# Cross attention: value products of four key tiles at a time, with twelve places for probabilities instead of two tiles and eight places

## The chip, the core and the metric

The kernel runs on one core of a Trainium2 chip. The metric is the device time of one execution in microseconds (us); lower is better. TensorE (PE) multiplies matrices into PSUM, VectorE (DVE) and ScalarE (ACT) read PSUM, GpSimd (POOL) works in SBUF only, SyncE (SP) issues transfers.

## The reference, cut to what matters

Four layers follow one another for a batch of 4, each with 256 tokens of width 256. The change lies in the third layer, in its cross attention with 16 heads of 8 dimensions over the 1601 context rows:

```
ci = rms_norm(hidden_states, ln_post_cross_w)
cq = heads(ci @ cq_w, NH, CHD)                      # 16 heads x 8
ck, cv = split(encoder_outputs @ ckv_w)             # encoder_outputs: 1601 rows x 128
scores = einsum('bhqd,bhkd->bhqk', q * scale, k)
p = softmax(scores, axis=-1)
cctx = einsum('bhqk,bhkd->bhqd', p, v)
hidden_states = hidden_states + cctx @ cdense_w
```

The batches are computed one after the other.

## The kernel before

The program is written out by hand, engine by engine, with semaphores between them. In the cross attention the 16 heads are worked in four groups of four (`gr` = 0 to 3), and the 1601 keys in 13 tiles of 128 (`KT` = 13). Within a group a key tile `kt` has two units (`u` = 0, 1), one for each two heads, so a group has 26 units, numbered `n` = 26 `gr` + 2 `kt` + `u`. In this text "score 11 of group 1" is unit 11 of that group.

For each unit, TensorE makes the scores, keys on partitions and 2 x 256 queries in the columns, in one matmul with a 128-column weight tile (`st<-cq_blocks,ck_stack`, or `x<-cq_blocks,ck_stack`) into one of three PSUM banks (`st_bank`). ScalarE takes the exponential into one of the places for probabilities (`slot(n)`: 4 in `prob`, 4 in `prob2`; in the profile `probs` and `probs_cross`). TensorE multiplies the probabilities with the values of the tile (`cross_pv`, `pv<-probs,v_cross` or `pv<-probs_cross,v_cross`), with weight tiles of 32 columns, into 32 partitions of `PV` for each head. One such float32 product stands as two rows in the trace, so the products of two key tiles are 16 rows and those of four tiles 32 rows.

The shift by the row maximum has to be known before a group starts. So behind every score matmul of group `gr` stands one matmul of another pass (`cross_max`, `x<-ck_stack,cq_blocks`), the scores of group `gr`+1 or `gr`+2 with queries on partitions, into one of three banks (`max_bank`), and VectorE reduces it (L1876, for the short last tile L1878). There are 26 of these for a group and they run 5 ahead (`LEAD`), so that the last one of all stands behind score 20 of group 2; group 3 has none.

In TensorE's order a step of the loop over `k0` takes two key tiles: four scores, each with its maximum matmul, and then the value products of the two tiles before. Other work stands in between:

- Queries: in groups 0 and 1, behind score 7, TensorE makes the query blocks of group `gr`+2 (`mi<-cq_hi,const_r`), and ScalarE copies them out behind exponential 7 (L794, four pieces).
- Shifts: before score 24 of groups 0 to 2, TensorE transposes the negated maxima (L1355), and ScalarE writes them into the query blocks (L801, four pieces) before its exponential 24. The next group's first score waits for them (`sc_set`).
- In group 3, behind score 11, four rows of a selector product (`x<-ctx_heads_t,const_f`) on the first three groups' results.
- A score waits for the exponential three units back, a maximum matmul for the reduction three back, and an exponential for a free place.

Of the kernel before, what the change touches and what calls it, by code (L numbers as in the profile page):

```python
# [15 lines left out]
F32 = mybir.dt.float32  # L16
# [7 lines left out]
P = 128  # L24
# [115 lines left out]
def program(nc, io):  # L140

    with ExitStack() as ctx:
        top = [nc.sbuf_base]

        def place(name, shape, dt, where):
            size = int(np.prod(shape[1:])) * (1 if dt == U8 else 4)
            off = -(-where[0] // 64) * 64
            where[0] = off + size
            return nc.alloc_sbuf_tensor_at(name, shape, dt, offset=off)

        def sb(name, shape, dt=F32):
            return place(name, shape, dt, top)
# [4 lines left out]
        def sig(name, per=1, primed=False):  # L157
            return Signal(ctx.enter_context(nc.semaphore(name)), per, primed)
# [20 lines left out]
        prob = sb("probs", [P, 4, 512])  # L179
        x0 = sb("x_in", [P, TT, D])  # L180
        xa, xb, xn = sb("x_a", [P, TT, D]), sb("x_b", [P, TT, D]), sb("x_normed", [P, TT, D])
# [82 lines left out]
        prob2 = place("probs_cross", [P, 4, 512], F32, e)  # L264
# [22 lines left out]
        wd = place("w_dense", [P, 2, 4, D], F32, w)  # L287
        z = [late]
        wgu = place("w_gate_up", [P, 2, DC, 2, FIP], F32, z)
        assert max(a[0], w[0], z[0]) <= nc.sbuf_usable_end  # L290


# [50 lines left out]
        sc_mm, pc_exp, pvc_mm = sig("sc_mm", 8 * KT), sig("pc_exp", 8 * KT, primed=True), sig("pvc_mm", 8 * KT, primed=True)  # L343
# [35 lines left out]
        def st_bank(n):  # L379

            return (ST[0][:], ST[1][:], half_bank(3))[n % 3]

        def slot(n):

            return prob[:, n % 8] if n % 8 < 4 else prob2[:, n % 8 - 4]

        block = ctx.enter_context(nc.Block())

# [210 lines left out]
        def _(act):  # L599
# [45 lines left out]
            def body(b, more):  # L645
# [143 lines left out]
                def cross_queries(gr):  # L789

                    act.wait_ge(qg_mm.handle, qg_mm.at(b * 4 + gr))
                    for h in range(4):
                        r = slice(32 * h, 32 * h + 32)
                        m = act.activation(qb2[gr % 3][r, h], MI[r, 0:NT], ACT.Identity, bias=ck[r, K_Q_CROSS:K_Q_CROSS + 1])  # L794
                    m.then_inc(qg_read.handle, 1)

                def cross_shifts(gr):

                    act.wait_ge(nmc_t.handle, nmc_t.at(b * 4 + gr))
                    for h in range(4):  # L800
                        m = act.activation(qb2[gr % 3][32 * h:32 * h + 4, h], MI[0:4, NT:2 * NT], ACT.Copy)  # L801
                    m.then_inc(sc_set.handle, 1)

                def cross_out(gr):

                    act.wait_ge(pvc_mm.handle, pvc_mm.at(b, 2 * KT * (gr + 1)))
                    act.activation(cx[:, gr], PV[:, 0:NT], ACT.Copy).then_inc(cc_read.handle, 1)
# [4 lines left out]
                for gr in range(4):  # L812
                    for k in range(2 * KT):
                        n = 2 * KT * gr + k
                        if gr < 3 and k == 24:
                            cross_shifts(gr + 1)
                        act.wait_ge(sc_mm.handle, sc_mm.at(b, n + 1))
                        act.wait_ge(pvc_mm.handle, pvc_mm.at(b, max(0, n - 7)))
                        act.activation(slot(n), st_bank(n), ACT.Exp, scale=float(HC2) ** -0.5).then_inc(pc_exp.handle, 1)  # L819
                        if gr and k == 3:  # L820
                            cross_out(gr - 1)
                        if gr < 2 and k == 7:
                            cross_queries(gr + 2)
# [10 lines left out]
            for b in range(B):  # L834
                body(b, b < B - 1)

        @block.tensor
        def _(pe):
            prime(pe, down_mm, sum_mm, pv_mm, pvs_mm, pvc_mm)
            def mm(out, lhsT, rhs, start=True, stop=True):  # L840
                return pe.matmul(out, lhsT, rhs, start=start, stop=stop, skip_group_check=True)  # L841
# [112 lines left out]
            def body(b, more):  # L954
# [264 lines left out]
                for m2 in range(2):  # L1219
                    for k in range(4):  # L1220
                        n = 0
# [5 lines left out]
                for t in range(TT):  # L1227
                    n = 0
# [105 lines left out]
                def cross_max(g):  # L1334

                    if g == 4 * CPARTS:
                        return
                    gr, m, bank = g // CPARTS, g % CPARTS, max_bank(g)
                    qt, h, c = m // 13, m % 13 // 3, m % 13 % 3
                    if m == 0:  # L1340
                        pe.wait_ge(qg_read.handle, qg_read.at(b * 4 + gr))
                    if g >= 3:
                        pe.wait_ge(mc2_read.handle, mc2_read.at(b, g - 2))
                    if m % 13 < 12:
                        t = mm(bank, qb2[gr % 3][:, h, qt * P:(qt + 1) * P], ks2[gr][:, c * 512:(c + 1) * 512])
                    else:
                        for h in range(4):
                            t = mm(bank[:, h * HEADW:(h + 1) * HEADW], qb2[gr % 3][:, h, qt * P:(qt + 1) * P], ks2[gr][:, 1536:1536 + HEADW])
                    t.then_inc(mc2_mm.handle, 1)

                def cross_shifts(gr):
                    pe.wait_ge(nmc.handle, nmc.at(b * 4 + gr))
                    pe.wait_ge(qg_read.handle, qg_read.at(b * 4 + min(gr + 1, 3)))
                    for qt in range(TT):
                        m = pe.transpose(MI[0:4, NT + qt * P:NT + (qt + 1) * P], nmx[:, qt, :], ident)  # L1355
                    m.then_inc(nmc_t.handle, 1)

                def cross_pv(gr, kt):

                    for u in range(2):  # L1360
                        n = 2 * KT * gr + 2 * kt + u
                        pe.wait_ge(pc_exp.handle, pc_exp.at(b, n + 1))
                        if kt == 0 and u == 0:
                            pe.wait_ge(cc_read.handle, cc_read.at(b * 4 + gr, 0))
                        for h in range(2):
                            hd = 2 * u + h
                            m = mm(PV[32 * hd:32 * hd + 32, 0:NT], vx[:, kt, VXW * (4 * gr + hd):VXW * (4 * gr + hd) + 32],
                                   slot(n)[:, h * NT:(h + 1) * NT], kt == 0, kt == KT - 1)
                        m.then_inc(pvc_mm.handle, 1)
# [7 lines left out]
                for gr in range(4):  # L1377
                    pe.wait_ge(sc_set.handle, sc_set.at(b * 4 + gr))
                    for k0 in range(0, KT, 2):
                        if k0 == 12 and gr < 3:  # L1380
                            cross_shifts(gr + 1)
                        for kt in range(k0, min(k0 + 2, KT)):
                            for u in range(2):
                                n = 2 * KT * gr + 2 * kt + u
                                pe.wait_ge(pc_exp.handle, pc_exp.at(b, max(0, n - 2)))
                                m = mm(st_bank(n), ks2[gr][:, kt * P:(kt + 1) * P],
                                       qb2[gr % 3][:, 2 * u:2 * u + 2].rearrange("p h n -> p (h n)"))
                                m.then_inc(sc_mm.handle, 1)
                                if g < 4 * CPARTS:
                                    cross_max(g)  # L1390
                                    g += 1
                        if gr < 2 and k0 == 2:
                            cross_queries(gr + 2)
                        if gr == 3 and k0 == 4:
                            pe.wait_ge(cc_read.handle, cc_read.at(b * 4 + 2))
                            mm(X[0][:, 0:512], cc[:, C_SELC], cx[:, 0:2].rearrange("p k n -> p (k n)"))
                            mm(X[0][:, 512:512 + NT], cc[:, C_SELC], cx[:, 2]).then_inc(cc_sum.handle, 1)
                        if k0:
                            cross_pv(gr, k0 - 2)
                            cross_pv(gr, k0 - 1)  # L1400
                        elif gr:
                            cross_pv(gr - 1, KT - 1)
                cross_pv(3, KT - 1)
                pe.wait_ge(cc_read.handle, cc_read.at(b * 4 + 3))
                mm(X[1][:, 0:NT], cc[:, C_SELC], cx[:, 3]).then_inc(cc_sum.handle, 1)
# [10 lines left out]
                for k in range(6):  # L1416
# [3 lines left out]
                    for gu in range(2):  # L1420
                        n = 0
# [6 lines left out]
                for t in range(TT):  # L1428
                    n = 0
# [10 lines left out]
            for b in range(B):  # L1440
                body(b, b < B - 1)
# [569 lines left out]
```

## Time and profile before

| | |
|---|---|
| median of 3 runs | 2308.95 us (2303.93 to 2312.57) |
| profiled execution, its own time | 2304.52 us |
| its span | 2302.7 us |
| TensorE busy | 87% |
| VectorE, ScalarE, GpSimd busy | 56%, 40%, 33% |
| mean granted TensorE clock | 0.921 |

The profile is of one execution. Its rows give the start from the beginning of the span, the duration, the engine, the line in the kernel, the operation and the tiles it writes and reads. "PEld" are the weight loads of TensorE, which can run beside its matmuls. Matmuls are pipelined, so the time that one costs is read from start to start, not from its duration.

### The profile page before, as it was taken

The page shows a single profiled execution, that of the slowest core. Times are in us where ns is not written, and L with a number is a line of the kernel's source. Part 1 is how long each engine was busy: PE and PEld are TensorE (multiplying, and loading weights), DVE is VectorE, ACT ScalarE, POOL GpSimd, SP SyncE. Part 2 cuts the span into 40 slices and gives each one's busy share as a digit, 9 for nine tenths or more (in the row PEclk, how much of TensorE's full clock was granted, in tenths as well). Part 3 has the DMA queues.
Part 4 walks back from the last instruction along what each step waited for, and adds up shares of the span by engine and source line. Part 5 has one row for each costly group of instructions (what it writes and reads, how often), then busy time and mean ns, then how long its engine had stood idle before and what let it go on. Part 6 is the DMA issues. An engine that isn't in the chain of part 4 may idle for free.

```text
span 2302.7 us, 30843 instructions
## 1 busy us (share of the span) xinstructions
PE 2004.1 (87%) x11940; PEld 1485.0 (64%) x11940; DVE 1298.0 (56%) x2045; ACT 923.0 (40%) x1718; POOL 766.9 (33%) x676
## 2 busy tenths in 40 slices
PE   3999888898899978899889988889888998888986
PEld 2676667556677657655676766765577765775655
DVE  5666335664676623675576753367457664346733
ACT  1455232371355413257045541326415553231731
POOL 3678410000378731000237881100025886100000
PEclk9999999799899999879999998988999999887998
DMA  4000200201000020100100001020010001102000
GB/s 177 9 11 5 112 1 1 83 1 43 29 12 8 12 104 1 42 41 1 48 26 14 8 37 76 1 83 1 23 36 20 10 8 69 44 1 82 1 1 5
DMA packets 18145, 74.16 MB, mean 32 GB/s; under 512 B 2896, under 2 KB 10320, under 8 KB 14544
## 3 DMA queue, kind: packets, MB, share of 16 engines
q1 hardware_dynamic: 17424, 69.56, 8.2%
q10 hardware_dynamic: 576, 2.62, 0.3%
q8 instruction: 96, 1.57, 0.3%
q14 instruction: 49, 0.40, 0.1%
HBM read 71.13 MB, written 1.05 MB: 31 GB/s over the span
## 4 chain that ended last, share of the span: by engine, by line
PE 68%; DVE 17%; ACT 7%; issue 5%; POOL 2%; DMA 1%; SPq 0%; ACTq 0%; POOLq 0%; DVEq 0%
PE x L841 27%; PE pv L841 18%; PE st L841 15%; PE mi L841 6%; DVE k_hi_lo L1459 3%; ACT k_hi_lo L612 2%; DVE max_parts L1540 2%; POOL prob_sums L555 1%; ACT probs L657 1%; DVE q_lo_shift L1549 1%; DVE prob_sums L1847 1%; PE x L965 1%; DVE x_normed L1640 1%; DVE w_pair_lo L1459 1%; ACT ck_stack L745 1%
## 5 line engine op out<-in xcount | busy, mean ns | idle before, releaser
L555 POOL TENSOR_TENSOR prob_sums<-prob_sums,probs 128x512 f32<-128x512 f32 x352 | 453.6, 1289 | 65.0 <-ACT probs L657 19.0
L657 ACT ACTIVATE probs<-st 128x512 f32<-128x512 f32 x416 | 228.5, 596 | 294.4 <-PE st L841 290.8
L1540 DVE TENSOR_REDUCE max_parts<-x 128x1 f32<-128x832 f32 x256 | 250.7, 1020 | 128.6 <-PE x L841 127.4
L539 POOL TENSOR_TENSOR rstd_work<-rstd_work 128x2 f32<-128x2 f32 x24 | 16.7, 695 | 796.4 <-DVE rstd_work L1456 796.4
L1876 DVE TENSOR_REDUCE max_cross<-x 128x1 f32<-128x512 f32 x384 | 238.8, 684 | 72.0 <-PE x L841 70.5
L841 PE MATMUL st<-q_hi_hi,k_hi_lo 128*128 128x256 f32 x832 | 231.2, 309 | 17.6 <-DVE q_lo_shift L1549 17.6
L841 PE MATMUL pv<-probs,v 128*64 128x256 f32 x1664 | 231.6, 397 | 3.7 <-DVE recip_sum L1664 3.7
L841 PEld LDWEIGHTS st<-q_hi_hi,k_hi_lo 128*128 128x128 f32 x832 | 159.9, 192 | 95.5 <-issue 86.2
L841 PE MATMUL st<-q_lo_shift,k_hi_rows 128*128 128x256 f32 x832 | 210.8, 285 | 0.0
L841 PE MATMUL x<-ck_stack,cq_blocks 128*128 128x512 f32 (+1 forms) x512 | 196.4, 458 | 0.1
L841 PEld LDWEIGHTS st<-q_lo_shift,k_hi_rows 128*128 128x128 f32 x832 | 160.7, 193 | 0.1
L1459 DVE TENSOR_TENSOR k_hi_lo<-x,k_hi_lo 64x832 fp32r<-64x832 f32 x128 | 131.0, 1023 | 40.6 <-ACT k_hi_lo L612 39.3
L841 PEld LDWEIGHTS pv<-probs,v 128*64 128x64 f32 x1664 | 101.1, 137 | 81.5 <-issue 27.1
L841 PE MATMUL x<-k_hi_rows,q_hi 128*128 128x416 f32 x512 | 128.9, 361 | 20.3 <-DVE k_hi_lo L1459 17.6
L841 PEld LDWEIGHTS x<-ck_stack,cq_blocks 128*128 128x128 f32 x512 | 107.6, 226 | 43.8 <-DVE max_cross L1876 32.2
L841 PE MATMUL st<-cq_blocks,ck_stack 128*128 128x512 f32 x280 | 121.6, 443 | 10.6 <-ACT cq_blocks L801 6.5
L1664 DVE RECIPROCAL recip_sum<-pv 128x256 f32<-128x256 f32 x32 | 56.2, 1757 | 108.8 <-PE pv L841 108.8
L612 ACT ACTIVATE k_hi_lo<-x 64x832 fp32r<-64x832 f32 x128 | 110.0, 859 | 17.6 <-PE x L841 15.9
L493 POOL TENSOR_SCALAR k_hi_rows<-k_hi_lo 64x1664 fp32r<-64x1664 f32 x64 | 101.0, 1579 | 38.6 <-ACT k_hi_lo L612 35.7
L841 PEld LDWEIGHTS x<-k_hi_rows,q_hi 128*128 128x128 f32 x512 | 85.3, 190 | 32.9 <-issue 28.9
L819 ACT ACTIVATE probs<-st 128x512 f32<-128x512 f32 x140 | 80.3, 604 | 28.4 <-PE st L841 27.9
L841 PEld LDWEIGHTS st<-cq_blocks,ck_stack 128*128 128x128 f32 x280 | 53.7, 194 | 56.5 <-ACT probs_cross L819 17.1
(291 smaller groups left out, 4158.0 us busy)
## 6 DMA issues: line engine op xcount, KB each, us to landing
w_gate_up<-in_wgu SPq DMA_DIRECT2D x4, 3072.0 KB, 10.1
w_ff<-in_w SPq DMA_DIRECT2D x8, 1024.0 KB, 5.7
w_qk<-in_wqk SPq DMA_DIRECT2D x4, 2048.0 KB, 9.0
w_pair<-in_w SPq DMA_DIRECT2D x32, 192.0 KB, 2.3
w_down<-in_wdn SPq DMA_DIRECT2D x4, 1536.0 KB, 13.4
w_dense<-in_wd SPq DMA_DIRECT2D x4, 1024.0 KB, 12.2
mask_ints<-in_mask SPq DMA_DIRECT2D x4, 832.0 KB, 4.3
ctx_t_raw<-in_ctxT SPq DMA_DIRECT2D x4, 832.0 KB, 5.3
```

The costliest lines, as they stand in the source:

```text
L493: pool.tensor_scalar(t["kh1"][0:64, :, c], r32(t["kst"][0:64, :, c]), 1.0, 0.0, ALU.mult, ALU.add)\
L555: pool.tensor_tensor(acc[:, 0], acc[:, 0], prob[:, kt % 4], ALU.add).then_inc(add_pool.handle, 1)
L612: act.activation(par[s]["kst"][0:64, h, j * HALF:(j + 1) * HALF].rearrange("p (c n) -> p c n", c=2), X[j][64 * h:64 * h + 64, :].rearrange ...
L657: act.activation(prob[:, kt % 4], ST[kt % 2][:], ACT.Exp, scale=HD0 ** -0.5).then_inc(p_exp.handle, 1)
L745: act.activation(ks2[gr][:, j * HALF:j * HALF + n], X[j][:, 0:n], ACT.Identity, bias=ck[:, K_OH_CROSS:K_OH_CROSS + 1])\
L819: act.activation(slot(n), st_bank(n), ACT.Exp, scale=float(HC2) ** -0.5).then_inc(pc_exp.handle, 1)
L841: return pe.matmul(out, lhsT, rhs, start=start, stop=stop, skip_group_check=True)
L965: last = pe.transpose(X[0][:, o:o + P], src[:, t, ch * P:(ch + 1) * P], ident)
L1459: return dve.tensor_tensor(out, x, y, op)
L1540: dve.tensor_reduce(mxs[:, qt, h, half:half + 1], X[n % 2][:].rearrange("p (c n) -> p c n", c=2)[:, :, 0:QUART], AX.XY, ALU.max).then_inc( ...
L1664: dve.reciprocal(rec[:], PV[:, NT:2 * NT]).then_inc(recip.handle, 1)
L1876: t = dve.tensor_reduce(mxc[:, qt, h, c:c + 1], bank, AX.X, ALU.max)
```

## The change

The value products are issued four key tiles at a time (behind the scores of tiles 5, 9 and 12) instead of two at a time (behind those of tiles 3, 5, 7, 9, 11 and 12). Those of tile 12 stay behind the first four scores of the next group. The places for probabilities grow from eight to twelve: two in a new tile `probs_cross_late`, and the tiles `x_in` (`x0`) and `x_normed` (`xn`), which nothing else uses during this stage. The exponential's wait for a free place goes from eight units back to twelve back.

```
@@ places @@
         wgu = place("w_gate_up", [P, 2, DC, 2, FIP], F32, z)
+        prob3 = place("probs_cross_late", [P, 2, 512], F32, z)
@@ slot(n) @@
-            return prob[:, n % 8] if n % 8 < 4 else prob2[:, n % 8 - 4]
+            n %= 12
+            if n < 8:
+                return prob[:, n] if n < 4 else prob2[:, n - 4]
+            return prob3[:, n - 8] if n < 10 else (x0, xn)[n - 10][:].rearrange("p t d -> p (t d)")
@@ ScalarE @@
                         act.wait_ge(sc_mm.handle, sc_mm.at(b, n + 1))
-                        act.wait_ge(pvc_mm.handle, pvc_mm.at(b, max(0, n - 7)))
+                        act.wait_ge(pvc_mm.handle, pvc_mm.at(b, max(0, n - 11)))
@@ TensorE @@
-                        if k0:
-                            cross_pv(gr, k0 - 2)
-                            cross_pv(gr, k0 - 1)
-                        elif gr:
+                        if k0 == 0 and gr:
                             cross_pv(gr - 1, KT - 1)
+                        if k0 and k0 % 4 == 0:
+                            for kt in range(k0 - 4, k0):
+                                cross_pv(gr, kt)
```

The first place is on TensorE in group 1, from the query blocks behind score 7 to score 12. Before, `cq_blocks_153` and `ck_stack_160` being this group's operands:

```order
L841 MATMUL mi<-cq_lo,const_r 128x256
L841 MATMUL pv<-probs,v_cross 32x256 x4
L841 MATMUL pv<-probs_cross,v_cross 32x256 x4
L841 MATMUL st<-cq_blocks_153,ck_stack_160 128x512
L841 MATMUL x<-ck_stack_161,cq_blocks_154 128x512
L841 MATMUL x<-cq_blocks_153,ck_stack_160 128x512
L841 MATMUL x<-ck_stack_161,cq_blocks_154 128x512
L841 MATMUL st<-cq_blocks_153,ck_stack_160 128x512
L841 MATMUL x<-ck_stack_161,cq_blocks_154 128x512
L841 MATMUL st<-cq_blocks_153,ck_stack_160 128x512
L841 MATMUL x<-ck_stack_161,cq_blocks_154 128x512
L841 MATMUL pv<-probs_cross,v_cross 32x256 x4
```

The same place in the changed program, where L845 is the same line four further down:

```order
L845 MATMUL mi<-cq_lo,const_r 128x256
L845 MATMUL st<-cq_blocks_153,ck_stack_160 128x512
L845 MATMUL x<-ck_stack_161,cq_blocks_154 128x512
L845 MATMUL x<-cq_blocks_153,ck_stack_160 128x512
L845 MATMUL x<-ck_stack_161,cq_blocks_154 128x512
L845 MATMUL st<-cq_blocks_153,ck_stack_160 128x512
L845 MATMUL x<-ck_stack_161,cq_blocks_154 128x512
L845 MATMUL st<-cq_blocks_153,ck_stack_160 128x512
L845 MATMUL x<-ck_stack_161,cq_blocks_154 128x512
L845 MATMUL pv<-probs,v_cross 32x256 x4
L845 MATMUL pv<-probs_cross,v_cross 32x256 x8
L845 MATMUL pv<-probs_cross_late,v_cross 32x256 x4
```

The products of tiles 0 and 1 have moved from ahead of score 8 to behind score 11 and its maximum matmul, where they now stand in front of those of tiles 2 and 3.

The second place is on ScalarE at the end of group 1, from exponential 20 to exponential 4 of group 2. Its order before:

```order
L819 ACTIVATE probs<-st 128x512 x2
L819 ACTIVATE probs<-x 128x512
L819 ACTIVATE probs<-st 128x512
L801 ACTIVATE cq_blocks_152<-mi 4x256 x4
L819 ACTIVATE probs_cross<-st 128x512
```

And in the changed program:

```order
L823 ACTIVATE probs<-st 128x512 x2
L823 ACTIVATE probs<-x 128x512
L823 ACTIVATE probs<-st 128x512
L805 ACTIVATE cq_blocks_152<-mi 4x256 x4
L823 ACTIVATE probs_cross<-st 128x512
```

Nothing has moved on ScalarE here or elsewhere in the stage: the exponentials only go to other places. VectorE's order is unchanged too.

## Rows read from the trace of the kernel before

**Rows 1.** The page: the chain that ended last, shares of the span by engine

```profile
PE 68%; DVE 17%; ACT 7%; issue 5%; POOL 2%; DMA 1%; SPq 0%; ACTq 0%; POOLq 0%; DVEq 0%
```

**Rows 2.** Stretches: length, busy PE, PEld, DVE, ACT, POOL, clock, DMA share, GB/s

```profile
400.00:404.00 4.00, 4.00 (x12) 3.21 (x12) 3.80 (x2) 0.00 (x0) 0.00 (x0) 0.60 0.00 0
...
448.00:526.00 78.00, 76.02 (x615) 42.86 (x613) 47.42 (x73) 60.93 (x124) 0.00 (x0) 1.00 0.01 1
...
1011.00:1089.00 78.00, 76.04 (x615) 42.90 (x614) 47.65 (x74) 60.93 (x124) 0.00 (x0) 1.00 0.00 1
```

**Rows 3.** Timeline of group 2, a step of two key tiles

```profile
496.54 0.40 PE L841 MATMUL st<-cq_blocks,ck_stack 128*128 128x512 f32 x1
496.78 0.40 PE L841 MATMUL x<-ck_stack,cq_blocks 128*128 128x512 f32 x1
497.11 1.07 PE L841 MATMUL pv<-probs_cross,v_cross 128*32 128x256 f32 x16
498.11 0.50 PE L841 MATMUL x<-cq_blocks,ck_stack 128*128 128x512 f32 x1
498.44 0.40 PE L841 MATMUL x<-ck_stack,cq_blocks 128*128 128x512 f32 x1
...
498.88 2.48 DVE L1876 TENSOR_REDUCE max_cross<-x 128x1 f32<-128x512 f32 x4 [0.58 <-PE x L841]
...
501.16 0.50 PE L841 MATMUL st<-cq_blocks,ck_stack 128*128 128x512 f32 x1
```

**Rows 4.** Timeline of group 1 from the query blocks to score 12

```profile
470.23 0.64 PE L841 MATMUL pv<-probs,v_cross 128*32 128x256 f32 x8
...
470.36 1.90 ACT L794 ACTIVATE cq_blocks<-mi,const_cols 32x256 fp32r<-32x256 f32 x4
...
472.29 0.60 ACT L819 ACTIVATE probs<-st 128x512 f32<-128x512 f32 x1
...
472.94 0.50 PE L841 MATMUL st<-cq_blocks,ck_stack 128*128 128x512 f32 x1
...
473.60 0.64 PE L841 MATMUL pv<-probs_cross,v_cross 128*32 128x256 f32 x8
474.06 0.61 PE L841 MATMUL pv<-probs,v_cross 128*32 128x256 f32 x8
474.60 0.50 PE L841 MATMUL x<-cq_blocks,ck_stack 128*128 128x512 f32 x1
```

**Rows 5.** VectorE's reductions (ns: shortest, median, longest), and seven in a row

```profile
L1876 DVE TENSOR_REDUCE max_cross<-x x384: 677/681/693, 422.6 to 2184.8; 128x1 f32<-128x512 f32 x192
...
465.87 4.52 DVE L1876 TENSOR_REDUCE max_cross<-x 128x1 f32<-128x512 f32 x7 [0.84 <-PE x L841]
```

**Rows 6.** A step of group 3, without maximum matmuls

```profile
517.57 0.50 PE L841 MATMUL st<-cq_blocks,ck_stack 128*128 128x512 f32 x1
...
518.11 0.60 ACT L819 ACTIVATE probs_cross<-st 128x512 f32<-128x512 f32 x1 [0.56 <-PE st L841]
...
518.76 0.50 PE L841 MATMUL st<-cq_blocks,ck_stack 128*128 128x512 f32 x1 [0.21 <-ACT probs_cross L819]
...
519.08 1.09 ACT L819 ACTIVATE probs<-st 128x512 f32<-128x512 f32 x2
519.19 0.64 PE L841 MATMUL pv<-probs,v_cross 128*32 128x256 f32 x8
...
520.19 0.50 PE L841 MATMUL x<-cq_blocks,ck_stack 128*128 128x512 f32 x1
```

**Rows 7.** From group 2 to group 3: shifts, then scores 0 and 4 of group 3

```profile
504.19 1.53 ACT L801 ACTIVATE cq_blocks<-mi 4x256 fp32r<-4x256 f32 x4 [0.24 <-PE mi L1355]
...
505.76 1.12 PE L841 MATMUL st<-cq_blocks,ck_stack 128*128 128x512 f32 x2
...
508.36 0.50 PE L841 MATMUL st<-cq_blocks,ck_stack 128*128 128x512 f32 x1
```

**Rows 8.** A wait of TensorE ahead of the stage

```profile
398.58 1.13 PE L841 MATMUL mi<-ctx_heads_t,const_f 128*128 128x512 f32 x2 [1.96 <-DVE ctx_heads_t L1853]
```

## The prediction

> **What bounds the kernel now.** I read the page's chain first. TensorE carries 68% of it, VectorE 17%, ScalarE 7% [rows 1]. That is a mean over unlike stages, so the stage that the change touches has to be read by itself. In its main stretch TensorE is busy for 76.02 of 78 us at the full granted clock, ScalarE for 60.93, VectorE for 47.42; the same stretch of the next batch reads 76.04 [rows 2]. So TensorE binds, ScalarE is not far behind, four batches repeat the same pattern, and what is worked out for one counts four times.
>
> Then the timeline of one step of two key tiles. Matmuls with 128-column weights start 0.23 to 0.24 apart, but the first value product starts 0.33 behind the last of them; eight product rows take 0.46 [rows 4], yet the block of sixteen is followed by the next score only after 1.00; and the matmul behind that score comes after 0.33 [rows 3]. A change between the two forms of weight tile and back thus costs 0.10 + (1.00 - 0.92) + 0.11 = 0.29 us a block. Check: 8 x 0.23 + 0.92 + 0.29 = 3.05, and the step reads 498.11 to 501.16.
>
> **The saving.** A group has seven product blocks now and four afterwards. Three blocks fewer x 0.29 x 16 groups = 13.9 us. That is the gain if TensorE never waits longer than before. The product rows, their number and their operands' sizes stay as they are; the new places are SBUF tiles like the old ones, with no transfer to or from them in this stage, and I cost them at nothing. Exponential n waits for the products of n - 12; at every step these are issued a block earlier than needed, so this wait never ends last.
>
> What it takes is cover. In a burst TensorE now makes eight scores and eight maximum matmuls at a stretch instead of four and four, with only three banks for each, so the readers' pace shows. And ScalarE's side jobs used to lie beside product blocks. Piece by piece, for a batch:
>
> *Scores 4 to 11 of groups 0 and 1.* ScalarE copies the query blocks for 1.90 us between exponentials 7 and 8. Exponential 8 starts at 472.29 and ends at 472.89, and score 11 starts at 472.94 [rows 4]. Before, 1.00 us of products (from 470.23) lay inside that wait; now scores 8 to 10 start there at once, TensorE is done with them at about 471.7 and stands still for about 1.2 us. Score 11 cannot come earlier, since ScalarE's chain has not moved. The block behind it still starts at 473.60, with 32 rows instead of 16, so score 12 comes 0.92 later than 474.60. The saved change is lost in the wait. Two groups: +1.84.
>
> *Scores 12 to 19 of groups 0 to 2.* A reduction lasts 0.68 [rows 5]; four in a row take 2.48, so they start (2.48 - 0.68) / 3 = 0.60 apart, the first one 0.77 behind the burst's first score [rows 3]. The eighth maximum matmul needs the fifth reduction's end: 0.77 + 4 x 0.60 + 0.68 + 0.05 for the hand-over = 3.90. Without that wait it would start at 0.33 + 7 x 0.46 = 3.55. So 0.35 is lost, and 0.10 more because its weights are loaded late, as behind any matmul that waited (518.76 to 519.19 is 0.43 instead of 0.33 [rows 6]). Less the 0.29 saved: +0.15 each, +0.45 for three.
>
> The Trainium skill warns of this kind of thing ("TensorEngine Tiling (Array Packing)", PSUM Bottleneck): faster TensorE work can leave the copying out of PSUM as the limit. The rows agree as far as 0.60 a reduction against 0.46 a pair of matmuls goes; by that rule taken alone, no burst could gain.
>
> *Scores 4 to 11 of group 2.* No queries, and one of its eight reductions is the short one: the full saving, -0.29.
>
> *Scores 20 to 25 of groups 0 to 2.* Groups 0 and 1: one block fewer, some 0.1 lost to reductions, -0.20 each, -0.40. In group 2 the longer block only covers the shifts, on which the next group's score 0 waits today (504.19 + 1.53 = 505.72, it starts at 505.76 [rows 7]): 0.
>
> *Group 3, no maximum matmuls.* ScalarE's pace binds. Its first four scores take 2.60 now [rows 7]; with the shifts and the last exponentials done under the longer block they take about 2.25, that is 0.33 x 3 for three scores, the wait for the fourth and a block of 8 rows: -0.35. A step reads 517.57 to 520.19, 2.62: the first exponential starts 0.54 behind the score, the third 0.97 later, so 0.485 apart; score 3 comes at +1.19, the block at +1.62 [rows 6]. In a burst of eight, score 7 comes at 1.19 + 4 x 0.48 = 3.11, the block at 3.54, the next score at 3.54 + 1.00 + 0.92 = 5.46 against 5.24 for two steps: +0.2 for each of two bursts. Here the products used to hide the latency of the first exponential twice and now do it once. The closing burst of six scores: score 5 at 2.15, block at 2.58, then five tiles' products 5 x 0.46 + 0.08 = 2.38, together 4.96 against 2.62 + 0.67 + 3 x 0.46 + 0.04 = 4.71: +0.25.
>
> **The sum.** 1.84 + 0.45 - 0.29 - 0.40 - 0.35 + 0.40 + 0.25 = +1.90 for a batch, +7.6 for four. The profiled execution took 2304.5 us, so it would take 2312.1. The median of the runs shown is 4.4 above that execution; at the median I forecast 2316. Bounds of its terms: the 0.92 is firm; the reductions' pace is 0.60 by one row and (4.52 - 0.68) / 6 = 0.64 by another that runs on without a gap [rows 5]; I take 0.60, since the seven may hold a wait. Groups' ends are good to 0.3 a batch or so. The forecast case thus spans +3 to +11 us.
>
> **Rivals.** A difference under 0.5% (11.5 us) is about what a measurement of this kernel cannot tell from no change.
>
> *A: the blocks' saving comes through, faster.* Place: the 48 changes of form that go. Price: 48 x 0.29 = 13.9 us, 2295. It decides if the exposed products behind the query copies are repaid, that is if the change of form costs well over 0.29 in places where its price is hidden in a wait now, or if readers keep up in the bursts. For it: 0.29 reads off nearly every step. Against it: score 11's wait is in the rows, and ScalarE's order is fixed. The Trainium skill ("TensorEngine Tiling (Array Packing)", Key Properties) says that changing the tiling mode drains TensorE, and so speaks for fewer changes; the 0.29 is this case's size of it. Half of this gain would land at -6, within the bound.
>
> *B: the readers' pace costs more.* At 0.64 a reduction, the 8-bursts lose 0.16 more each: three of them +0.48, group 2's first one and the two ends about +0.35. Then +2.7 a batch, +11. At 0.68, no overlap between reductions, 5 x 0.68 - 4 x 0.60 - 0.68 = 0.32 more per burst and all ends at nought: 3.6 a batch, +14. I price it at +13, 2322. For it: the seven-row chain. Against it: most rows of four give 0.60.
>
> *C: TensorE's clock falls in the new waits.* After a wait of 1.96 us [rows 8] the stretch from 400 to 404 us ran at 0.60 of the full clock [rows 2], between the two levels of 1.2 and 2.4 GHz. The new waits are about 1.2 us, two in each batch. If each cost 4 us at the lower level, that stretch would do 2 us of full-speed work; I take 1.7 as lost, since a part lies in the readers' waits: 8 x 1.7 = 14 on top of 7.6, +21, 2330. Against it: the wait is shorter, and the stage's clock is full through its waits of today, such as the 0.21 at 518.76 [rows 6].
>
> *D: nothing changes.* Excluded as an order: the products stand elsewhere. Without the four more places it could not even run, since exponential 8 would wait for products that stand behind score 11.
>
> **How the numbers follow.** Forecast case 0.60; half of A (-6 to +3) 0.06; A 0.11; B 0.13; C 0.10. Faster by over 0.5%: A, 0.11. Slower by over 0.5%: B and C, 0.23. Within: 0.66. The range leaves out A's full gain and the upper part of C: 2301 to 2329; the likeliest case alone runs from 2311 to 2321.
>
> **What would show it.** Right: product blocks of 32 rows, three a group; score 11 of groups 0 and 1 still 0.05 behind the end of exponential 8 with about 1.2 us of idle TensorE ahead of it; idle TensorE ahead of the last maximum matmuls of a burst, released by L1876; two steps of group 3 near 5.46; the stretch from the first group's result to the last 1.5 to 2 us longer in each batch; the clock at 1.00 in it. Wrong: a shorter stretch (the change of form was worth more, or the reductions kept up), a clock under 1.00 in it, or time moving in a stage that the change does not touch.

## The result, and the profile after

The changed kernel takes 2313.59 us (median of 20 runs, 2309.68 to 2320.0), the kernel before 2305.16 us in the same comparison (20 runs, 2302.74 to 2315.52): a ratio of 1.003, 95% interval 1.002 to 1.004. The medians are 8.4 us apart and the means 7.2; the interval of the ratio is 4.6 to 9.2 us. The profiled execution of the changed kernel took 2317.1 us with a span of 2315.3, so it lies 3.5 above its median, and the difference of the two profiled spans (12.6) overstates the change. Of the 12 executions of the kernel before with added matmuls of constants (below), one took 2835.66 us at a mean granted clock of 0.637 and is left out of its ratio.

To read the stage I measure from the first shift copy of a batch (L801, now L805) to the last group's result (L807, now L811). In the changed kernel's timeline of ScalarE, batch 0:

```profile
440.67 1.52 ACT L805 ACTIVATE cq_blocks<-mi 4x256 fp32r<-4x256 f32 x4 [16.86 <-PE mi L1359]
...
526.35 0.38 ACT L811 ACTIVATE ctx_heads_t<-pv 128x256 f32<-128x256 f32 x1 [1.47 <-PE pv L845]
```

That is 85.68 us from start to start. The kernel before has 84.21:

```profile
440.94 1.53 ACT L801 ACTIVATE cq_blocks<-mi 4x256 fp32r<-4x256 f32 x4 [16.84 <-PE mi L1355]
...
525.15 0.38 ACT L807 ACTIVATE ctx_heads_t<-pv 128x256 f32<-128x256 f32 x1 [0.72 <-PE pv L841]
```

Batches 1 and 2 give the same within 0.05; in batch 3 both are shorter, 83.87 against 82.35, because the first scores find TensorE at its high clock there (granted 1.00 in the first 3 us of the stage, against 0.50 in the other three batches; scores 0 to 4 take 1.94 us instead of 3.58). The stage grew by 1.46 to 1.52 in each of the four: 5.9 us in all.

The timeline of group 1, which answers to [rows 4]:

```profile
470.59 0.39 PE L845 MATMUL st<-cq_blocks,ck_stack 128*128 128x512 f32 x1
...
470.81 1.90 ACT L798 ACTIVATE cq_blocks<-mi,const_cols 32x256 fp32r<-32x256 f32 x4
...
472.74 0.60 ACT L823 ACTIVATE x_in<-st 128x512 f32<-128x512 f32 x1
...
473.39 0.50 PE L845 MATMUL st<-cq_blocks,ck_stack 128*128 128x512 f32 x1 [1.24 <-ACT x_in L823]
...
474.05 0.64 PE L845 MATMUL pv<-probs,v_cross 128*32 128x256 f32 x8
474.51 1.05 PE L845 MATMUL pv<-probs_cross,v_cross 128*32 128x256 f32 x16
475.37 0.61 PE L845 MATMUL pv<-probs_cross_late,v_cross 128*32 128x256 f32 x8
475.92 0.51 PE L845 MATMUL x<-cq_blocks,ck_stack 128*128 128x512 f32 x1
```

Score 8 starts at once behind the query blocks, score 11 waits 1.24 us idle for exponential 8 (it starts 0.05 behind that one's end, 472.74 + 0.60), and the products of four tiles stand behind it. From score 4 (468.19) to score 12 it takes 7.73 us; before it took 6.87.

The eight-score burst behind it:

```profile
476.70 4.88 DVE L1880 TENSOR_REDUCE max_cross<-x 128x1 f32<-128x512 f32 x8 [1.84 <-PE x L845]
...
479.24 0.19 PEld L845 LDWEIGHTS x<-ck_stack,cq_blocks 128*128 128x128 f32 x1 [0.30 <-DVE max_cross L1880]
479.24 0.50 PE L845 MATMUL x<-ck_stack,cq_blocks 128*128 128x512 f32 x1
...
479.57 0.39 PE L845 MATMUL st<-cq_blocks,ck_stack 128*128 128x512 f32 x1
...
479.83 0.50 PE L845 MATMUL x<-ck_stack,cq_blocks 128*128 128x512 f32 x1
...
482.13 0.50 PE L845 MATMUL st<-cq_blocks,ck_stack 128*128 128x512 f32 x1
```

Eight reductions run in a chain, (4.88 - 0.68) / 7 = 0.60 apart, and the last three maximum matmuls (478.64, 479.24 and 479.83) have rows of 0.50, each behind a weight load that waited 0.30 for a maximum. Score 12 to score 20 is 6.21 us, against 6.11 for two steps before. The list of who waited for whom says the same for the whole kernel (us, number of waits, longest wait), first of the kernel before, then of the changed one:

```profile
PEld x L841 <- DVE max_cross L1876: 32.2, 92, 0.7
```

```profile
PEld x L845 <- DVE max_cross L1880: 45.3, 140, 0.7
```

In the stage's main stretch, which answers to [rows 2], the granted clock is 1.00; TensorE is a little less busy (74.84 of 78 us instead of 76.02). The second row is a stretch just behind the stage, where it is not:

```profile
448.00:526.00 78.00, 74.84 (x612) 43.31 (x610) 46.78 (x73) 59.31 (x121) 0.00 (x0) 1.00 0.01 1
...
529.00:536.00 7.00, 6.21 (x15) 4.95 (x16) 0.70 (x2) 0.00 (x0) 0.00 (x0) 0.51 0.00 0
```

The output products in that stretch, first of the kernel before, then of the changed one:

```profile
528.59 5.41 PE L841 MATMUL x<-w_cd,ctx_heads_t 128*128 128x256 f32 x16 [2.31 <-DVE ctx_heads_t L1459]
```

```profile
529.79 6.76 PE L845 MATMUL x<-w_cd,ctx_heads_t 128*128 128x256 f32 x16 [2.31 <-DVE ctx_heads_t L1463]
```

The same sixteen rows behind the same wait of 2.31 us take 1.35 us longer. From the last group's result to the first silu it is 24.0 us in batches 0 to 2, 22.4 before (batch 3: 22.6 against 21.2). This code did not change. The silu of batch 0, before and after:

```profile
547.53 0.38 ACT L830 ACTIVATE silu<-x 128x256 f32<-128x256 f32 x1 [20.70 <-PE x L841]
```

```profile
550.35 0.38 ACT L834 ACTIVATE silu<-x 128x256 f32<-128x256 f32 x1 [22.32 <-PE x L845]
```

### The profile page after: what moved, and what is told of

It reads as the page before. It is cut to its first block, busy times and chain, and to the rows that moved or that the text cites. A ratio compares the mean times of both kernels' runs of the same rounds, so it can differ in the third digit from the quotient of the medians.

```text
span 2315.3 us, 30843 instructions
## 1 busy us (share of the span) xinstructions
PE 2007.9 (87%) x11940; PEld 1489.6 (64%) x11940; DVE 1297.8 (56%) x2045; ACT 920.0 (40%) x1718; POOL 763.6 (33%) x676
## 4 chain that ended last, share of the span: by engine, by line
PE 68%; DVE 17%; ACT 7%; issue 6%; POOL 2%; DMA 1%; SPq 0%; ACTq 0%; POOLq 0%; DVEq 0%
PE x L845 27%; PE pv L845 17%; PE st L845 15%; PE mi L845 6%; DVE k_hi_lo L1463 3%; ACT k_hi_lo L616 2%; DVE max_parts L1544 1%; POOL prob_sums L559 1%; ACT probs L661 1%; DVE q_lo_shift L1553 1%; DVE prob_sums L1851 1%; PE x L969 1%; ACT cq_blocks L798 1%; DVE x_normed L1644 1%; DVE w_pair_lo L1463 1%
## 5 line engine op out<-in xcount | busy, mean ns | idle before, releaser
L661 ACT ACTIVATE probs<-st 128x512 f32<-128x512 f32 x416 | 227.8, 596 | 292.1 <-PE st L845 288.5
L845 PE MATMUL st<-q_hi_hi,k_hi_lo 128*128 128x256 f32 x832 | 227.8, 306 | 17.3 <-DVE q_lo_shift L1553 17.3
L845 PE MATMUL pv<-probs,v 128*64 128x256 f32 x1664 | 231.7, 397 | 3.7 <-DVE recip_sum L1668 3.7
L845 PEld LDWEIGHTS st<-q_hi_hi,k_hi_lo 128*128 128x128 f32 x832 | 157.4, 189 | 95.1 <-issue 85.8
L845 PE MATMUL st<-q_lo_shift,k_hi_rows 128*128 128x256 f32 x832 | 207.9, 282 | 0.0
L845 PE MATMUL x<-ck_stack,cq_blocks 128*128 128x512 f32 (+1 forms) x512 | 200.5, 466 | 0.1
L845 PEld LDWEIGHTS st<-q_lo_shift,k_hi_rows 128*128 128x128 f32 x832 | 158.2, 190 | 0.1
L845 PEld LDWEIGHTS pv<-probs,v 128*64 128x64 f32 x1664 | 101.3, 137 | 81.7 <-issue 27.5
L845 PE MATMUL x<-k_hi_rows,q_hi 128*128 128x416 f32 x512 | 129.7, 363 | 20.1 <-DVE k_hi_lo L1463 17.6
L845 PEld LDWEIGHTS x<-ck_stack,cq_blocks 128*128 128x128 f32 x512 | 107.5, 226 | 57.3 <-DVE max_cross L1880 45.3
L845 PE MATMUL st<-cq_blocks,ck_stack 128*128 128x512 f32 x280 | 122.3, 444 | 13.4 <-ACT cq_blocks L805 6.4
L845 PEld LDWEIGHTS x<-k_hi_rows,q_hi 128*128 128x128 f32 x512 | 85.5, 191 | 33.0 <-issue 29.2
L845 PEld LDWEIGHTS st<-cq_blocks,ck_stack 128*128 128x128 f32 x280 | 54.1, 194 | 53.2 <-ACT x_in L823 10.2
L579 POOL TENSOR_TENSOR ck_lo<-ck,ck_hi 128x416 fp32r<-128x416 f32 x16 | 16.7, 1064 | 182.6 <-ACT ck L694 182.6
## 6 DMA issues: line engine op xcount, KB each, us to landing
w_gate_up<-in_wgu SPq DMA_DIRECT2D x4, 3072.0 KB, 10.1
```

Source lines behind the costliest of these rows:

```text
L661: act.activation(prob[:, kt % 4], ST[kt % 2][:], ACT.Exp, scale=HD0 ** -0.5).then_inc(p_exp.handle, 1)
```

## The experiments

**Query copies later.** The wait of score 11 is taken away by moving the copies, not the wait:

```
 # TensorE
-                        if gr < 2 and k0 == 2:
+                        if gr < 2 and k0 == 4:
                             cross_queries(gr + 2)
 # ScalarE
-                        if gr < 2 and k == 7:
+                        if gr < 2 and k == 11:
                             cross_queries(gr + 2)
```

> The changed kernel, with the query blocks of group gr+2 made behind score 11 (ahead of the four-tile product block) and copied by ScalarE behind exponential 11, instead of behind score 7 and exponential 7. The stage length is counted from the first shift copy to the last group's result of a batch: 84.2 us in the kernel before, 85.7 in the changed one. Theory 1 (the products that used to lie beside the query copies stand behind score 11 now, and that is what the change costs): scores 4 to 12 of group 1 take about 6.2 us instead of 7.7, of group 0 about 6.7 instead of 8.25, the stage 82.7 to 83.0, and the time falls to about 3 to 6 us under that of the kernel before. Rival (long bursts cost by themselves, wherever the copies stand): scores 4 to 12 of group 1 stay above 7.3 and the stage above 85.

Measured: 2304.91 us against 2309.72 of the kernel before on the same chip, ratio 0.9979 (0.9966 to 0.9992). Its timeline of group 1:

```profile
467.56 0.50 PE L845 MATMUL st<-cq_blocks,ck_stack 128*128 128x512 f32 x1
...
471.90 0.64 PE L845 MATMUL pv<-probs,v_cross 128*32 128x256 f32 x8
472.24 1.90 ACT L798 ACTIVATE cq_blocks<-mi,const_cols 32x256 fp32r<-32x256 f32 x4
...
473.76 0.50 PE L845 MATMUL x<-cq_blocks,ck_stack 128*128 128x512 f32 x1
```

Score 4 to score 12 is 6.20 us (6.79 in group 0), and the copies lie beside the product block. The stage is 82.60 and 82.54 us in batches 0 and 1. So the wait behind the query copies costs 3.1 us a batch, more than twice what the whole change costs. Without it the change of form pays.

**The same move without the change.** The kernel before, two tiles at a time, with that edit alone.

> The kernel before, eight places and two tiles at a time, with only the query blocks and their copies moved behind score 11 and exponential 11. Theory 1 (the gain of the later copies comes from the four-tile block, whose 1.9 us cover the copies' 1.90; a two-tile block of 1.0 us does not): groups 0 and 1 stay within 0.3 us of today's and the stage at 83.7 to 84.5 us. Rival (the copies stood badly anyway, and moving them is worth the same in either form): stage below 83.2.

One execution: the stage is 84.46 and 84.49 us in batches 1 and 2, against 84.21. From its timeline of group 1:

```profile
470.81 0.50 PE L841 MATMUL x<-cq_blocks,ck_stack 128*128 128x512 f32 x1
...
474.38 0.50 PE L841 MATMUL st<-cq_blocks,ck_stack 128*128 128x512 f32 x1
```

These two are scores 12 and 16. Scores 4 to 12 take 6.49 instead of 6.87, but the next step takes 3.57 instead of 3.04, since the copies now reach out from under the block of 1.0 us: score 15, at 472.72, waits 0.25 for an exponential. In the stage the move pays only together with blocks of four tiles. The single time, 2302.08 against 2309.4, lies lower than this stage explains; one execution does not settle 7 us here, since the lengths of unchanged code differ by as much (last section).

**Group 3 in twos.** The changed kernel with

```
-                        if k0 and k0 % 4 == 0:
+                        if gr < 3 and k0 and k0 % 4 == 0:
                             ...
+                        if gr == 3 and k0:
+                            cross_pv(gr, k0 - 2)
+                            cross_pv(gr, k0 - 1)
```

> The changed kernel, with the products of group 3 alone in blocks of two key tiles again. Theory 1 (in group 3 ScalarE's pace binds, and a long block hides the latency of the first exponential only once where two hid it twice): two steps of group 3 take 5.24 us again instead of 5.44, the closing part 0.2 less, the stage 85.1 instead of 85.7, and the time is 2 us under that of the changed kernel, so 6 above the kernel before. Rival (group 3 gains from fewer blocks as the others do): the stage grows over 85.7.

Measured: 2306.41 us, ratio to the kernel before 0.999 (0.998 to 1.0). The stage is 85.11, 85.14 and 85.13 us, 0.55 less than in the changed kernel. In its timeline two steps of group 3 take 5.23 us again (the first row is two scores, the first of them score 12; the second is score 20):

```profile
516.58 0.73 PE L845 MATMUL st<-cq_blocks,ck_stack 128*128 128x512 f32 x2
...
521.81 0.50 PE L845 MATMUL x<-cq_blocks,ck_stack 128*128 128x512 f32 x1
```

The mechanism and its size in the stage hold. The total does not follow: I expected it 6 us above the kernel before, and it came out 3.3 below. In the profiled execution the piece from the result to the silu is 21.35 us in batches 0 to 2 and not 24.0, with the output products at 5.35 instead of 6.76. That is 2.65 a batch through the clock, more than the 0.55 of the stage.

**One tile at a time.** The kernel before, with the products of tile kt - 2 behind the two scores of tile kt.

```
+                            if kt >= 2:
+                                cross_pv(gr, kt - 2)
+                            elif gr:
+                                cross_pv(gr - 1, KT - 2 + kt)
 ...
+                cross_pv(3, KT - 2)
                 cross_pv(3, KT - 1)
```

> The kernel before, with eight places, and the products of one key tile at a time (twelve blocks a group instead of six, besides the last tile's). Theory 1 (a change between 128-column and 32-column weight tiles and back costs 0.29 us on TensorE's own path): the four steps in a row of group 2 grow from 3.05 to 3.63 each, groups 0 to 2 by 1.7 us each, group 3 by nothing since ScalarE binds there: stage 89.4 instead of 84.2, time 20 us up. Rival A (the price of the change of form is well over 0.29 and partly hidden now): steps over 3.8. Rival (the gaps are only room that TensorE has anyway): steps stay 3.05.

One execution: 2326.57 us. Scores 12, 14 and 16 of group 2 with one of the blocks between them:

```profile
496.67 0.50 PE L841 MATMUL st<-cq_blocks,ck_stack 128*128 128x512 f32 x1
...
497.80 0.64 PE L841 MATMUL pv<-probs_cross,v_cross 128*32 128x256 f32 x8
498.37 0.50 PE L841 MATMUL st<-cq_blocks,ck_stack 128*128 128x512 f32 x1
...
500.06 0.50 PE L841 MATMUL x<-cq_blocks,ck_stack 128*128 128x512 f32 x1
```

Two tiles take 3.39 us instead of 3.05. The 3.63 that I had written was a slip: a step gets one more block, not two, so 0.29 more was due, and 0.34 came. In the three batches that begin at the high clock the stage is 87.52 us against 82.35 for such a batch of the kernel before, 5.2 more, as the sum over groups said. By groups it is +0.9, +2.1, +2.6 and -0.4 where the sum had 1.7 for each of the first three and nothing for the last, so that agreement is in part luck. A change of form and back costs about 0.3 us on TensorE's path, and rival A's "well over 0.29" is out.

**Half reductions.** The changed kernel, in which VectorE reads 256 of the 512 columns (the maxima over the other half are left out):

```
-                            t = dve.tensor_reduce(mxc[:, qt, h, c:c + 1], bank, AX.X, ALU.max)
+                            t = dve.tensor_reduce(mxc[:, qt, h, c:c + 1], bank[:, 0:256], AX.X, ALU.max)
```

> The changed kernel, in which VectorE reduces only the first 256 columns of each full maximum bank (the maxima of the other half of the keys are left out), so that a reduction takes about 0.4 us instead of 0.68. Theory 1 (the last maximum matmuls of an eight-score burst wait for the reductions' pace): scores 12 to 20 take 5.8 to 5.9 us instead of 6.2 in groups 0 to 2, no stalled matmul stands in these bursts, stage 84.6 instead of 85.7. Rival (the bursts are as long as TensorE's own work makes them): 6.2 stays and the stage 85.7.

One execution, scores 12 and 20 of group 1 and the eight reductions between:

```profile
466.32 0.50 PE L845 MATMUL x<-cq_blocks,ck_stack 128*128 128x512 f32 x1
...
467.10 3.67 DVE L1880 TENSOR_REDUCE max_cross<-x 128x1 f32<-128x256 f32 x8 [2.11 <-PE x L845]
...
472.10 0.50 PE L845 MATMUL st<-cq_blocks,ck_stack 128*128 128x512 f32 x1
```

The burst takes 5.78 us instead of 6.21, as expected, and no weight load in the burst waits for a maximum. The stage, in four batches that all begin at the high clock, is 82.2 us against 83.9 in such a batch of the changed kernel, 1.7 less where I expected 1.1. So the reductions' pace takes 0.43 there, more than the 0.29 that the saved block brings. The Trainium skill's warning that reading PSUM out may become the limit once TensorE is faster ("TensorEngine Tiling (Array Packing)", PSUM Bottleneck) is borne out in these bursts, by that 0.43. The total, 2282.56 us, fell far more than I expected: the 37 rows of maximum matmuls ahead of the stage, which go at the reductions' pace as well, shrank from 18.5 to 12.3 us in batch 0. I had counted the bursts alone.

**Places alone.** Twelve places, two tiles at a time.

> The kernel before with the twelve places alone, products two tiles at a time as before. Theory 1 (no exponential ever waits for a place last, and the new tiles cost nothing): stage 84.2 us in the first three batches, as before, group by group within 0.1. Rival (the new places cost or give something, for instance by where they lie): the stage moves by over 0.3.

One execution, 2301.63 us: stage 84.22 and 84.24 us in batches 0 and 1, 82.37 and 82.35 in the others, the groups within 0.1; output products 5.41 and 5.11 to 5.14 us. The places cost nothing, in the stage or behind it.

**The best order.** Later copies, four tiles at a time in groups 0 to 2, two in group 3.

> Four tiles at a time in groups 0 to 2, two at a time in group 3, and the query copies behind exponential 11. Theory 1 (the two losses are independent: 3.1 us a batch behind the query copies, 0.55 in group 3): stage 85.68 - 3.1 - 0.55 = 82.0 us against 84.2 of the kernel before, 2.2 a batch or 8.8 in all, time about 0.4% under the kernel before, give or take the 3 us that the clock's falls behind the stage move it by. Rival (the losses overlap): stage 82.5 or more.

Measured: 2290.78 us against 2306.84, ratio 0.9926 (0.9908 to 0.9945). The stage is 82.10 and 82.11 us in the batches that begin at the low clock: the two losses are independent. That is 2.1 a batch, 8.4 in all. The total fell by 16, twice that and more than the 9, give or take 3, that I expected. In the profiled execution, 13.5 below that of the kernel before, the stage holds 10.1 of it, because one more batch began at the high clock; the other 3.4 lie in code that did not change.

**A held clock behind the stage.** Constants are multiplied into a free bank during the wait of 2.31 us, in the kernel before and in the changed one:

```
                 mm(X[1][:, 0:NT], cc[:, C_SELC], cx[:, 3]).then_inc(cc_sum.handle, 1)
+                for _ in range(9):
+                    mm(ST[0][:], cr[:, R_ID], cr[:, R_SELF:R_SELF + 4].rearrange("p k n -> p (k n)"))
```

> The kernel before with nine matmuls of constants into a free bank (2 us) behind the last selector product, where TensorE waits 2.3 us for VectorE's reciprocal at each batch's end of the stage. Theory 2 (this wait lets the granted clock fall to half in the output products behind it, for a time that depends on where the fall comes): the sixteen rows of x<-w_cd take about 3.5 us instead of 5.4 and read a clock of 1.00; from the last result to the first silu 20 us instead of 22.4; time 6 to 9 us under the kernel before. Rival (the fall has another cause): no change.

> The changed kernel with the same nine matmuls of constants. Theory 2: the output products take 3.5 us here too instead of 6.8, so the part of the difference that lies behind the stage (22.4 against 24.0 us from the last result to the first silu) goes, and this kernel lies above the warmed kernel before by the stage alone: 4 x 1.47 = 5.9 us. Rival (the changed kernel slows what follows by something else, such as its places in x_in): a difference of 1.6 a batch stays behind the stage.

Measured: the warmed kernel before 2303.15 us, ratio 0.9983 (0.9969 to 0.9998); the warmed changed kernel 2309.1, ratio 1.0003 (0.9989 to 1.0017). In the timeline of the warmed kernel before:

```profile
528.88 2.41 PE L841 MATMUL st<-const_r 128*128 128x512 f32 x9
531.53 3.72 PE L841 MATMUL x<-w_cd,ctx_heads_t 128*128 128x256 f32 x16 [0.24 <-DVE ctx_heads_t L1461]
...
542.37 1.84 PE L841 MATMUL x<-x_v_t,w_gate_up 128*128 128x256 f32 x4 [2.42 <-DVE x_l_t L1461]
```

The output products take 3.72 us instead of 5.41, at a granted clock of 1.00, so in the kernel before it is behind this idle wait that the clock is low. But only 3.7 us reached the total (0.5 to 7 by the interval) of the 6 to 9 expected. In that execution the piece from the result to the silu is 2.66 shorter in batches 0 to 2, and the distance from one batch's result to the next is 563.23 and 563.21 us, against 563.23 and 559.80. The gain is lost again in code that did not change: from the first silu of batches 0 to 2 to the next stage it is 459.3, 459.2 and 459.1 us at a mean granted clock of 0.91, against 456.6, 453.2 and 456.4 at 0.92, 0.93 and 0.92 in the kernel before. The profiled execution as a whole is 6.3 us longer than that of the kernel before.

The medians of the two warmed kernels are 5.95 us apart, and the stage gives 5.6 in their profiled executions. That agreement is no proof, because each median is uncertain by some 3 us. The output products are 3.72 us in both, and yet a difference stays behind the stage. Their silus of batch 0 (results at 528.09 and 527.38), of the warmed kernel before and of the warmed changed one:

```profile
547.81 0.38 ACT L830 ACTIVATE silu<-x 128x256 f32<-128x256 f32 x1 [18.04 <-PE x L841]
```

```profile
548.21 0.38 ACT L834 ACTIVATE silu<-x 128x256 f32<-128x256 f32 x1 [19.15 <-PE x L845]
```

That is 19.7 against 20.8 us in batches 0 to 2, and the other way round in batch 3. So these two kernels do not show the stage to be the whole difference. Against the rival, that the changed kernel itself slows what follows, speak other executions: the places alone did not; the kernel before with nothing but later query copies also has output products of 6.62 us and 23.8 us to the silu in batch 0; and batch 3 of the changed kernel has output products of 5.41.

**Both.** The best order with these nine matmuls and ten more behind the transposes of the MLP's input.

> The kernel with later copies, four tiles at a time in groups 0 to 2 and two in group 3, plus matmuls of constants in two waits behind the stage: nine behind the last selector product and ten behind the transposes of the MLP's input. Theory 2 as the warmed kernels left it (the clock can be held through such a wait, but a batch's length falls back on a few values, so that a part of what is gained there is lost at later waits): output products 3.5 us, first MLP products at full clock, from the last result to the first silu 17 us or less instead of 21.2 to 22.6, and of these 4 us a batch at most half reach the total: 2283 to 2289 us. Rival (all of it reaches the total): 2275 or less. Rival (none does): 2291.

Measured: 2283.72 us against 2309.4, ratio 0.9883 (0.9865 to 0.9901). From the result to the silu it is 18.04 us in every batch, where I expected 17 or less, and the granted clock is 1.00 there:

```profile
529.00:536.00 7.00, 5.72 (x28) 4.54 (x27) 3.81 (x12) 0.00 (x0) 0.70 (x1) 1.00 0.51 178
536.00:545.00 9.00, 8.88 (x41) 7.41 (x41) 2.66 (x5) 0.69 (x2) 0.00 (x0) 1.00 0.00 0
```

## Why the prediction was right

- **The saving of 0.29 a block** held: 0.34 by one tile at a time, and -0.26 against -0.29 for scores 4 to 12 of group 2, where nothing else binds.
- **Scores 4 to 11 of groups 0 and 1**, +0.92 each: +0.83 and +0.86, with 1.24 us of idle TensorE where I had about 1.2. This was the main term, and moving the copies shows it to be the cause.
- **Scores 12 to 19**, +0.15 each: +0.12, +0.10, +0.09. The reductions keep 0.60, so rival B's pace did not come.
- **Groups' ends**, -0.20 each: -0.23 and -0.17; in group 2 +0.05.
- **Group 3**: the first four scores -0.41 (predicted -0.35), the bursts +0.19 and +0.20 (+0.2 each), the end, from score 20 to the result, +0.09 (+0.25).
- **The sum** was +1.90 a batch; the stage shows +1.47. The end of group 3 was 0.16 too high; no other term was wrong by over 0.1, but most of them were a little too high, and they add up.
- **What I had not in the sum**: the code behind the stage. My sign of error, "time moving in a stage that the change does not touch", came true: in the profiled execution the output products and what follows add 1.4 to 1.7 us a batch through the clock. The runs' medians differ by 8.4, the stage by 5.9; the interval of 4.6 to 9.2 holds the stage alone, so how much of the rest is real is left open. That the +7.6 of the sum lies so near the 8.4 of the medians is in part luck: the stage was put 1.7 us too high, and what came behind it was put at nothing.
- **Rival C** did not come: the granted clock reads 1.00 from 470 to 477 us, through the idle 1.24 us.
- **Rival A** did not come, for the reason named against it. With the copies out of the way and group 3 in twos, 8.4 us do come through in the stage, of the 10.4 that the 36 blocks saved there are worth at 0.29.

## What to carry to other kernels

Fewer switches between forms of work save only what no other engine's pace takes back: before making a run longer, list what lay beside each short piece, here ScalarE's 1.90 us of copies, and move that too. Where three banks stand between a producer and a reader, a longer run is paid at the reader's pace. Measure such a change by the stage's own length in the trace; here the total moved by as much again in code that did not change, at another granted clock.

## What the runs showed of the hardware that I had not expected

- The same wait of 2.31 us is followed by a low clock of different length, or by none. In the kernel before the granted clock reads 0.73 from 529 to 530 us, 0.56 from 532 to 533 and 1.00 from 533 on; in the changed kernel it is 0.57 from 529 to 530 and still 0.51 from 534 to 536. The output products take 5.41 or 6.76 us accordingly. In the last batch of the kernel with group 3 in twos they take 3.72 behind the same wait, at a granted clock of 1.00:

```profile
2221.13 3.72 PE L845 MATMUL x<-w_cd,ctx_heads_t 128*128 128x256 f32 x16 [2.31 <-DVE ctx_heads_t L1466]
```

- From one batch's last result to the next, the same code takes 559.80, 561.10 or 563.23 us in one execution of the kernel before, and 563.20, 564.71 or 566.57 in one of the changed kernel. So what is gained at one place can be lost elsewhere: the warmed kernel before gained 2.66 us behind each of its first three results and took 2.6, 6.0 and 2.7 more from there to the next stage.
- Matmuls of constants in a wait hold the clock: in all four batches of each of the three warmed kernels the sixteen rows take 3.72 us.
